# The last matrix product of a dense layer: FP32 against three fp32r products of parts, one stage later in a software pipeline

## The reference

```
o = o.reshape(b, n, n, D) @ W_out
h = layer_norm(x + o, ln_agg_g, ln_agg_b)
m = jax.nn.relu(h @ W1 + b1) @ W2 + b2
return layer_norm(m + h, ln2_g, ln2_b)
```

## Time and profile before

| | us |
|---|---|
| median of 3 runs | 3816.36 |
| the profiled execution's own time | 3818.34 |
| its span | 3816.5 |
| PE busy, whole span | 3493.4 (92%) |
| DVE, ACT, POOL busy | 2918.6, 2444.4, 1309.3 |
| dense stage, about | 1097.6 to 1430 |

### The profile page before, as it was taken

How to read it: one execution, slowest core, us unless ns; L and a number is a source line. 1 busy time by engine, 2 the same in 40 slices (tenths; PEclk the granted TensorE clock), 3 DMA queues, 4 the chain that set the end, 5 groups by cost and what they waited for, 6 DMA issues and landing times. The chain is left out here.

```text
span 3816.5 us, 81795 instructions
## 1 busy us (share of the span) xinstructions
PE 3493.4 (92%) x30707; PEld 2953.6 (77%) x30707; DVE 2918.6 (76%) x4371; ACT 2444.4 (64%) x6220; POOL 1309.3 (34%) x735
## 2 busy tenths in 40 slices
PE   8878888888879988999999989999999979899987
PEld 7755555555559977888888878888888878788886
DVE  4679999999968865777777766777777767677887
ACT  4548888888855545666666655666666633677775
POOL 0009999999955541000000001000000024222254
PEclk9989999999989989999999999999999989999999
DMA  5674111211124321000000010000000046555575
GB/s 147 196 207 108 44 39 44 64 41 44 39 69 135 118 93 46 18 18 17 18 18 12 12 53 17 18 18 17 18 18 12 12 153 211 170 144 143 143 227 166
DMA packets 199348, 294.39 MB, mean 77 GB/s; under 512 B 17920, under 2 KB 155520, under 8 KB 195968
## 3 DMA queue, kind: packets, MB, share of 16 engines
q1 hardware_dynamic: 189824, 282.08, 24.7%
q10 hardware_dynamic: 9216, 8.39, 0.6%
HBM read 197.87 MB, written 92.54 MB: 76 GB/s over the span
## 5 line engine op out<-in xcount | busy, mean ns | idle before, releaser
L737 POOL TENSOR_TENSOR mx_big<-mp_lvs,mx_big 128x1280 f32<-128x1280 f32 (+1 forms) x224 | 709.9, 3239 | 282.3 <-ACT mp_lvs L657 277.5
L712 DVE TENSOR_TENSOR mx_big<-mp_psL,mx_big 128x2816 f32<-128x2816 f32 (+1 forms) x224 | 691.4, 3145 | 21.2 <-PE mp_psO L602 18.3
L664 ACT ACTIVATE mp_cut<-mp_psO,mx_mask 128x128 f32<-128x128 f32 x2048 | 553.1, 405 | 140.1 <-PE mp_psO L602 110.2
L602 PE MATMUL mp_psO<-mx_big,mp_pair 128*16 128x256 f32 x8192 | 498.5, 383 | 110.8 <-DVE mx_big L712 84.9
L1538 PE MATMUL sv_psO<-at_v_hi,sv_p_hi 128*128 128x258 f32 x2048 | 584.0, 285 | 13.5 <-DVE sv_p_lo L1626 10.3
L1557 ACT ACTIVATE sv_S<-sv_psS,at_kb 128x512 f32<-128x512 f32 x512 | 353.0, 689 | 372.1 <-PE sv_psS L1512 294.3
L1538 PE MATMUL sv_psO<-at_v_lo,sv_p_hi 128*128 128x258 f32 x2048 | 578.6, 282 | 0.0
L1538 PE MATMUL sv_psO<-at_v_hi,sv_p_lo 128*128 128x258 f32 x2048 | 577.7, 282 | 0.0
L1601 DVE TENSOR_TENSOR sv_run<-sv_run,sv_S 128x512 f32<-128x512 f32 x448 | 313.3, 699 | 289.2 <-ACT sv_S L1557 289.2
L602 PEld LDWEIGHTS mp_psO<-mx_big,mp_pair 128*16 128x16 f32 x8192 | 324.7, 127 | 249.2 <-DVE mx_big L712 136.9
L1538 PEld LDWEIGHTS sv_psO<-at_v_hi,sv_p_hi 128*128 128x128 f32 x2048 | 386.2, 189 | 43.1 <-DVE sv_p_lo L1626 21.1
(11 more groups left out here) (288 smaller groups left out, 7724.1 us busy)
## 6 DMA issues: line engine op xcount, KB each, us to landing
re_xg<-xg SPq DMA_DIRECT2D x192, 384.0 KB, 3.3
xg<-ga_xg SPq DMA_DIRECT2D x32, 768.0 KB, 4.0
att<-mx_big SPq DMA_DIRECT2D x16, 1024.0 KB, 6.7
mp_pair<-att SPq DMA_DIRECT2D x128, 128.0 KB, 2.9
mx_big<-rv SPq DMA_DIRECT2D x14, 1024.0 KB, 11.9
fr_xr<-in_x SPq DMA_DIRECT2D x16, 512.0 KB, 4.7
fr_xl<-in_x SPq DMA_DIRECT2D x32, 256.0 KB, 4.2
rv<-fr_rvs SPq DMA_DIRECT2D x16, 512.0 KB, 3.2
```

Source lines behind the costliest of these rows:

```text
L602: mm = pe.matmul(psO[32 * j:32 * j + 2 * H, c % 2, q, :], pair[:, s, :, :, c * YC + y], Z[:, c % 2, y, :], start=True, stop=True, tile_pos ...
L664: ins = nc.scalar.activation(cut[:, s, c, :, h * DK:(h + 1) * DK], psO[:, c % 2, :, h * DK:(h + 1) * DK], ACT.Copy, scale=mask[:, h:h + 1])
L712: nc.vector.tensor_tensor(Z[:, c % 2, 0:m], psL[:, s, 0:D].unsqueeze(1).broadcast_to([P, m, D]), rv_place(big, seventh, b, c)[:, 0:m], ALU ...
L737: nc.gpsimd.tensor_tensor(Z[:, c % 2, m:YC], lvs[:, s, :].unsqueeze(1).broadcast_to([P, YC - m, D]), rv_place(big, seventh, b, c)[:, m:YC] ...
```

## The change

The outer layer becomes a product of parts. `wb` is cut once into `wb_hi` (ScalarE) and `wb_lo` (GpSimd). For each tile ScalarE rounds the Relu's result from SBUF into `mT_hi`, right behind its Relu and ahead of `xl`. GpSimd then makes the rest, `mT_lo`, as its last step of the iteration. The outer layer moves from tile i-2 to tile i-3. All that follows it (the second and the third norm, `xT`, the stores) moves by one iteration too, and LAST goes from NT+5 to NT+6. `hb` gets a fifth slot. The iterations of `turn_weights`, `fold` and the `kw` work stay at NT+1, NT+2 and NT+3.

```diff
-    LAST = NT + 5
+    LAST = NT + 6
@@ tensor
+                def outer(n):
+                    pe.wait_ge(wb_cut, 1)
+                    pe.wait_ge(mT_kept, n + 1)
+                    reach(pe, added3, n)
                     for u in range(U):
-                        for k in range(blocks):
-                            mm = pe.matmul(dst[:, u * D:(u + 1) * D], lhsT[:, k, u * P:(u + 1) * P], w[:, k, :], start=(k == 0), stop=(k == blocks - 1))
-                    mm.then_inc(done, 1)
+                        terms = [t for k in range(MT) for t in parts(k)]
+                        for e, (a, c, k) in enumerate(terms):
+                            mm = pe.matmul(ps_3[:, u * D:(u + 1) * D], mTs[a][:, n % 2, k, u * P:(u + 1) * P], wbs[c][:, k, :],
+                                           start=(e == 0), stop=(e == len(terms) - 1))
+                    mm.then_inc(made3, 1)
...
-                    n = i - 2
+                    n = i - 3
                     if 0 <= n < NT:
-                        pe.wait_ge(mT_made, n * 2 + 2)
-                        reach(pe, added3, n)
-                        by_token(ps_3, mT[:, n % 2], wb, MT, made3)
-                    n = i - 5
+                        outer(n)
+                    n = i - 6
@@ scalar
                 keep_oT_hi(0)
+                nc.scalar.copy(wb_hi[:, :, :], wb[:, :, :]).then_inc(wb_hi_cut, 1)
...
                         act.wait_ge(b1_made, 1)
+                        reach(act, mT_kept, n - 1)
...
-                    n = i - 4
+                    n = i - 1
+                    if 0 <= n < NT:
+                        act.wait_ge(mT_made, n * 2 + 2)
+                        reach(act, made3, n - 1)
+                        nc.scalar.copy(mT_hi[:, n % 2], mT[:, n % 2]).then_inc(mT_hi_kept, 1)
+                    n = i - 5
                     if 0 <= n < NT:
                         act.wait_ge(xoff_made, n + 1)
@@ vector
-                    n = i - 3
+                    n = i - 4
                     if 0 <= n < NT:
                         dve.wait_ge(made3, n + 1)
                         dve.wait_ge(hb_made, n + 1)
-                        nc.vector.tensor_tensor(t0[:, n % 2], tiles(ps_3), hb[:, n % 4], ALU.add).then_inc(added3, 1)
+                        nc.vector.tensor_tensor(t0[:, n % 2], tiles(ps_3), hb[:, n % 5], ALU.add).then_inc(added3, 1)
@@ gpsimd
+                pool.wait_ge(wb_hi_cut, 1)
+                nc.gpsimd.tensor_tensor(wb_lo[:, :, :], wb[:, :, :], wb_hi[:, :, :], ALU.subtract).then_inc(wb_cut, 1)
...
+                    n = i - 1
+                    if 0 <= n < NT:
+                        pool.wait_ge(mT_hi_kept, n + 1)
+                        reach(pool, made3, n - 1)
+                        nc.gpsimd.tensor_tensor(mT_lo[:, n % 2], mT[:, n % 2], mT_hi[:, n % 2], ALU.subtract).then_inc(mT_kept, 1)
```

More of the change, by code:

```diff
@@ L877, in dense_layers @@
         mT = ph.sb("mT", [P, 2, MT, W])
+        mT_hi, mT_lo = (ph.sb(n, [P, 2, MT, W], F32R) for n in ("mT_hi", "mT_lo"))
+        wb_hi, wb_lo = (ph.sb(n, [P, MT, D], F32R) for n in ("wb_hi", "wb_lo"))
         hg = ph.sb("hg", [P, 2, U, D])
-        hb = ph.sb("hb", [P, 4, U, D])
+        hb = ph.sb("hb", [P, 5, U, D])
         t0 = ph.sb("t0", [P, 2, U, D])
@@ L904, in dense_layers @@
         w_hi_cut, w_cut, b1_turned, b1_made = (ph.sem(n) for n in "w_hi_cut w_cut b1_turned b1_made".split())
+        wb_hi_cut, wb_cut, mT_hi_kept, mT_kept = (ph.sem(n) for n in "wb_hi_cut wb_cut mT_hi_kept mT_kept".split())
         made1, made2, made3 = ph.sem("made1"), ph.sem("made2"), ph.sem("made3")
@@ L992, in parts @@
                     return ((0, 0, k), (0, 1, k), (1, 0, k))
-                def by_token(dst, lhsT, w, blocks, done):
+                def outer(n):
+                    pe.wait_ge(wb_cut, 1)
+                    pe.wait_ge(mT_kept, n + 1)
+                    reach(pe, added3, n)
                     for u in range(U):
-                        for k in range(blocks):
-                            mm = pe.matmul(dst[:, u * D:(u + 1) * D], lhsT[:, k, u * P:(u + 1) * P], w[:, k, :], start=(k == 0), stop=(k == blocks - 1))
-                    mm.then_inc(done, 1)
+                        terms = [t for k in range(MT) for t in parts(k)]
[3 more added lines that the diff above has]
+                    mm.then_inc(made3, 1)
+                mTs, wbs = (mT_hi, mT_lo), (wb_hi, wb_lo)
                 oTs, wos, hTs, was = (oT_hi, oT_lo), (wo_hi, wo_lo), (hT_hi, hT_lo), (wa_hi, wa_lo)
@@ L1262, in _ @@
                         pool.wait_ge(h_scaled, i + 1)
-                        reach(pool, added3, i - 3)
-                        nc.gpsimd.tensor_tensor(hb[:, i % 4], hg[:, i % 2], both(hbr), ALU.add).then_inc(hb_made, 1)
+                        reach(pool, added3, i - 4)
+                        nc.gpsimd.tensor_tensor(hb[:, i % 5], hg[:, i % 2], both(hbr), ALU.add).then_inc(hb_made, 1)
+                    n = i - 1
[3 more added lines that the diff above has]
+                        nc.gpsimd.tensor_tensor(mT_lo[:, n % 2], mT[:, n % 2], mT_hi[:, n % 2], ALU.subtract).then_inc(mT_kept, 1)
 def attention_phase(nc, b, t_d, xlT_d, wqT, bq, wkT, bk, wvT, bv, ident_d, t2_d):
```

1 line of the change is left out of this document (removed).

## The result

The changed kernel takes 3838.12 us (median of 5 runs, 3836.39 to 3838.58). The kernel before, timed beside it, takes 3816.36 (5 runs, 3815.67 to 3819.65). The ratio is 1.0054, with a 95% interval from 1.0041 to 1.0068. Forecast were 3824.4 and a range of 3812 to 3831. The direction was right, and the cost was 21.8 us instead of 8.

The account below looks back on a forecast made before the run. TensorE bounds the kernel at 9.02 us a period; a ring of waits at 9.09 takes its place. -2.5 up to the last inner layer and +10.5 at the end give +8.0: 3826.3 profiled, 3824.4 median; range 3812 to 3831.

Parts of the forecast that it names:

- the ring: Steady dense stage: Relu, cast, xl, hT_hi, VectorE's chain, transposes and TensorE, over two periods: 18.18, so 9.09 us each.
- The margin is 0.53 us: Steady period before: VectorE ends hn at 8.49 us, TensorE wants it at 9.02.
- so I take nothing: GpSimd's mT_lo, 2.56 us, delays tg and ts by up to 0.7; ts is read an iteration later: no cost.
- a period over 9.3 would speak for GpSimd: Sign in the profile after: a steady period over 9.3 us would point to GpSimd slowing VectorE.
- Steady part: Dense stage's 24 steady periods: 0.07 us more each, 1.7 us in all.
- Removed from TensorE: Outer layer per tile: 3.34 us down to 2.84, so TensorE's own period falls from 9.02 to 8.52.
- The cast: ScalarE's mT_hi between Relu and xl: 1.04 us, moving xl and VectorE's chain up to hn by 1.11.
- The rival: GpSimd's mT_lo stretches VectorE's chain by 0.5 us, 0.25 more a period, 7 us over 27: 3831; chance 0.15.
- Start: Start of the dense stage's pipeline: 3.4 us ahead after iteration 6, as iteration 2 has no outer layer.
- End: Last inner layer to last xT: 37.2 us in place of 26.7, one more iteration of latency, +10.5.

Follow-up runs that it names:

- cast alone: Kernel before plus ScalarE's cast of mT per tile into a buffer nobody reads, outer layer still FP32: 3827.12 us, ratio 1.0029.
- no rest: Changed kernel without GpSimd's mT_lo per tile (zeros filled once, cast still made): 3833.82 us, ratio 1.0044.
- the run with the root moved: Changed kernel with the root of the third norm behind the four Relus on ScalarE instead of ahead of them: 3837.71 us, ratio 1.0054.
- inner layer first, no rest: Changed kernel, old lags, outer layer behind inner on TensorE, third norm's root behind the Relus, mT_lo zero: 3804.38 us, ratio 0.9970.
- the lag alone: Kernel before with the FP32 outer layer and all behind it one iteration later, no cast or mT_lo: 3825.94 us, ratio 1.0022.

## Why the prediction was wrong

**The failed step is the ring.** "The ring spans two periods: 9.66 + 8.52 = 18.18, so 9.09 us a period." I followed the release of the Relu through TensorE only and did not ask what else stands ahead of it on ScalarE. Root X does, and it waits for the end of the same VectorE chain that the Relu sets off by way of `hT_hi`. That ring closes in one period, so a cast on it counts whole and not by half. Before, it was hidden. Relu's second pair waited 0.52 us for TensorE, which left the ring 0.65 of slack (four Relus took 1.55 once they ran without a wait, and 2.20 from 1248.57 to 1250.77 before; these are ScalarE's rows of the kernel before, root X first).

```profile
1248.31 0.30 ACT L1095 ACTIVATE de_std<-de_mv,de_eps 128x2 f32<-128x2 f32 x1 [0.43 <-DVE de_mv L1165]
1248.57 0.84 ACT L1145 ACTIVATE de_mT<-de_ps_m,de_b1s 128x256 f32<-128x256 f32 x2
1249.93 0.84 ACT L1145 ACTIVATE de_mT<-de_ps_m,de_b1s 128x256 f32<-128x256 f32 x2 [0.52 <-PE de_ps_m L1083]
```

Its own length was 9.02 - 0.65 = 8.37. With the cast's 1.02 (1.05 less the early start of its successor) it is 9.39. That is what cast alone (9.391) and no rest (9.395) measured. I had written: "The margin is 0.53 us." The slack of the ring that mattered was 0.65, and 1.02 went over it: 9.39 - 9.02 = 0.37 us a period in place of 0.07.

**The second failed step is GpSimd, put at nothing.** I had looked at how late `tg` and `ts` would be and written "so I take nothing". `mT_lo` holds `tn`, and with `hg` and `hb` this makes a ring of 9.44 us by itself. It is as long as the whole measured period (9.455), so GpSimd's ring alone would have given the same steady part, as the run with the root moved shows (9.459). My own sign for it came true: a period over 9.3 would speak for GpSimd.

**Steady part.** Predicted +0.07 a period and 1.7 us. Measured +0.44. Ring A alone gives 0.37 of it and the ring through GpSimd alone all of it; the two do not add. From the 6th `hg` to the 32nd this was +11.2 us, 9.5 more than predicted, out of a miss of 13.7.

**Removed from TensorE.** Right: 24 matmuls from 1409.81 to 1412.77, 2.96 us, 0.12 apart as taken. TensorE's own period fell from 9.02 to 8.58 (inner layer first, no rest), 0.44 for the 0.50 predicted. Saved, but idled away.

**The cast.** Right in size: 1.05 us for 1.04.

**GpSimd.** The estimate of 2.56 for `mT_lo` was 2.40. The rival was dismissed with the earlier trace rows, and this was weak evidence. The sum with `hb` has one operand in PSUM, and `tn`, the instruction that is held, never ran beside GpSimd before, because GpSimd was waiting for it. The prediction also counted operands of "one tensor only" among those that show no stretch; `tn` reads one tensor, and it is the one held. The rival named the right pair of engines, but as a stretch of 0.25 a period, not as a ring. What the rest costs depends on what else stands beside it: 0.06 a period with ring A in place (9.455 against 9.395), 0.43 with ring A cut (9.459 against 9.026), 0.84 with the inner layer first (9.419 against 8.581). `tn` on its tile before and after (ns min/median/max):

```profile
L1173 DVE TENSOR_SCALAR de_tn<-de_t,de_mv,de_rstd x64: 405/410/415, 1136.2 to 1411.0; 128x256 f32<-128x256 f32 x64
```

```profile
L1187 DVE TENSOR_SCALAR de_tn<-de_t,de_mv,de_rstd x64: 400/411/1994, 1141.8 to 1438.8; 128x256 f32<-128x256 f32 x64
```

The median hides it, and the maximum shows it: 30 of the 64 began beside `mT_lo` and took 440 ns or more.

**Start.** Taken at -3.4 up to iteration 6, measured -1.4. From the 1st `hg` to the 6th the kernel before took 42.2 us, the lag alone 38.9, no rest 38.7 and the changed kernel 40.4. So without GpSimd's rest this stretch came out near the prediction, 3.5 shorter than before, and the rest cost 1.8 of it: the two first halves of `tn` that met `mT_lo` there took 0.88 us (at 1141.82) and 1.99 (at 1149.82) in place of 0.41. With 26 steady periods at 0.06, 1.6 us, this is most of the 4.3 us that the version without the rest gains in all.

**End.** Right in its mechanism and near in size. The last `xT` ends 38.6 us behind the last inner layer (1409.0 to 1447.62) for 37.2, so +11.9 for the +10.5 predicted. The 1.4 too little are there when the last outer layer is done: `fold` starts at 9.0 for 8.3, that outer layer ends at 21.5 for 19.9, and the layer itself took 4.76 for 4.6 at the lower clock. 3.8 us are the `fold` and `kw` work in front of it, as the move of it showed. The two halves of the answer had the right mechanism at the end and the wrong one in the middle.

## What to carry to other kernels

An engine that is 100% busy hides every ring of waits that is shorter than its own work. Before work is taken off it, list for each instruction on the other engines not only who releases it but what stands ahead of it in its engine's order and what that waits for, and divide the length of each closed loop by the periods that it spans: here a root ahead of a Relu made the loop one period long instead of two. Where two rings are almost equally long, cutting one shows nothing, so cut each alone and both together before calling a ring harmless. To see what a neighbour costs an engine, look for the very instruction that will overlap, and at its maximum, not its median. Evidence from another form, or from one that never overlapped, did not decide it here.
